# Half of the columns of the middle pass's row additions, moved from VectorE to GpSimd

## The reference, cut to what matters

```
terms = [x, L @ x]
for _ in range(2, 4):
    terms.append(2.0 * (L @ terms[-1]) - terms[-2])
out = einsum('kni,kio->no', stack(terms), weight)
```

```
deg = maximum(adj.sum(axis=1, keepdims=True), 1e-08)
```

## Time and profile before

| | us |
|---|---|
| median of 3 runs | 1737.84 |
| profiled execution | 1742.45 |
| its span, first to last instruction | 1740.6 |
| TensorE busy | 1542.5 (89%) |
| VectorE busy | 1250.4 (72%) |
| ScalarE busy | 947.7 (54%) |
| GpSimd busy | 297.3 (17%) |

### The profile page before, as it was taken

How to read it: one execution, slowest core, us unless ns; L and a number is a source line. 1 busy time by engine, 2 the same in 40 slices (tenths; PEclk the granted TensorE clock), 3 DMA queues, 4 the chain that set the end, 5 groups by cost and what they waited for, 6 DMA issues and landing times.

```text
span 1740.6 us, 21314 instructions
## 1 busy us (share of the span) xinstructions
PE 1542.5 (89%) x8169; PEld 653.1 (38%) x8214; DVE 1250.4 (72%) x1609; ACT 947.7 (54%) x920; POOL 297.3 (17%) x150
## 2 busy tenths in 40 slices
PE   6999989999999699999999997788788888888880
PEld 1433333333333344444444444233333333333330
DVE  4677699986888656747749654456567888888877
ACT  1233477753344433324343344656567999999964
POOL 1000000000000000000000002675224444444430
PEclk9999999999999799999999998999678999999995
DMA  9999599938999335333334302346124444544410
GB/s 349 412 413 413 213 357 381 392 130 316 413 413 381 115 146 193 147 146 146 145 135 156 145 1 73 121 133 218 37 97 133 148 155 136 186 163 158 136 46 24
DMA packets 118109, 348.99 MB, mean 201 GB/s; under 512 B 6324, under 2 KB 31224, under 8 KB 117752
## 3 DMA queue, kind: packets, MB, share of 16 engines
q1 hardware_dynamic: 106784, 329.27, 50.9%
q10 hardware_dynamic: 11224, 18.36, 2.8%
HBM read 329.78 MB, written 17.83 MB: 200 GB/s over the span
## 4 chain that ended last, share of the span: by engine, by line
PE 52%; issue 18%; DVE 13%; POOL 13%; ACT 2%; DMA 2%; SPq 0%; POOLq 0%; DVEq 0%; ACTq 0%
PE ps L741 13%; PE ps L863 13%; POOL ring L635 11%; PE ps L869 9%; DVE work L1611 4%; PE ps L674 3%; DVE work L1648 3%; PE ps L673 3%; PE ps L892 2%; POOL work L615 2%; PE ps L808 2%; DMA ring<-in_adjT 2%; PE ps L705 1%; PE ps L898 1%; DVE work L1624 1%
## 5 line engine op out<-in xcount | busy, mean ns | idle before, releaser
L615 POOL TENSOR_SCALAR work<-work 128x1024 int16<-128x1024 uint8 x32 | 97.0, 3041 | 1106.2 <-DMA work<-codes 1044.5
L863 PE MATMUL ps<-ring,X 128*64 128x512 f32 x512 | 264.0, 597 | 13.3 <-DVE ring L1867 13.3
L1134 ACT ACTIVATE work<-ps,code_bias 128x1024 uint8<-128x1024 f32 x128 | 135.8, 1111 | 247.7 <-PE ps L674 239.2
L864 PE MATMUL ps<-work,X 128*64 128x512 f32 x512 | 264.0, 597 | 0.0
L1255 ACT ACTIVATE work<-ring 128x2048 f32<-128x2048 f32 x64 | 122.2, 1911 | 222.0 <-PE ps L871 201.1
L635 POOL TENSOR_TENSOR ring<-ring,work 128x1024 f32<-128x1024 f32 x80 | 189.8, 2372 | 280.8 <-DVE work L2092 280.6
L871 PE MATMUL ps<-work 128*64 128x512 bf16 x768 | 208.2, 380 | 0.0
L869 PE MATMUL ps<-work 128*64 128x512 bf16 x768 | 208.2, 380 | 0.0
L958 PE MATMUL ps<-work 96*128 96x512 f32 x320 | 169.5, 655 | 0.0
L741 PE MATMUL ps<-ring,work 128*64 128x512 f32 x704 | 161.7, 601 | 0.0
L1864 DVE TENSOR_SCALAR work<-ring 128x2048 bf16<-128x2048 f32 x64 | 78.5, 1226 | 106.0 <-PE ps L871 105.8
(11 more groups left out here) (316 smaller groups left out, 2766.0 us busy)
## 6 DMA issues: line engine op xcount, KB each, us to landing
ring<-in_adjT SPq DMA_DIRECT2D x90, 2048.0 KB, 10.6
work<-in_adjT SPq DMA_DIRECT2D x26, 2048.0 KB, 12.0
ring<-in_adjT SPq DMA_DIRECT2D x48, 1024.0 KB, 7.7
codes<-work ACTq DMA_DIRECT2D x64, 256.0 KB, 6.1
work<-codes SPq DMA_DIRECT2D x32, 512.0 KB, 3.6
ring<-in_adjT SPq DMA_DIRECT2D x32, 512.0 KB, 3.6
X<-in_x ACTq DMA_DIRECT2D x1, 1024.0 KB, 6.9
work<-in_xT SPq DMA_DIRECT2D x2, 512.0 KB, 22.6
```

The source lines that it names most:

```text
L615: nc.gpsimd.tensor_scalar(decay[i % 2][:, 3, :].rearrange("p (h c) -> p h c", h=2), code_in[:, i % RING, :, 3, :], 128.0, None, ALU.mult). ...
L863: nc.tensor.matmul(ps[0:F, h, :], rows, ring[:, r, k, cols], start=start, stop=stop)
L864: nc.tensor.matmul(ps[F:P, h, :], rows, negs[:, pair, i, cols], start=start, stop=stop)
L1134: nc.scalar.activation(codes[:, u, k:k + 2, :].rearrange("p k c -> p (k c)"), ps[:, bank:bank + 2, :].rearrange("p k c -> p (k c)"), ACT.Relu,
```

## The change

In the middle pass VectorE adds columns 0 to 511 of each block and GpSimd columns 512 to 1023 (`ADD_COLS = HALF`), each to its own columns of the sums. GpSimd's additions stand in its program behind the constants. Each waits for its tile and for its own addition before; the first of all also waits for VectorE's 32 additions of the first pass. SP waits for GpSimd's additions too before it loads into a slot, and VectorE's first addition of the third pass waits for all 64. The semaphores of the square roots of the first two layers are merged into one.

```diff
@@ SP, wait_for_last_use
                 if t >= SLOTS:
                     sp.wait_ge(tile_signed, min(t + 1 - SLOTS, SLOTS))
+                    sp.wait_ge(pool_added, 2 * min(t + 1 - SLOTS, SLOTS))
@@ GpSimd, behind the constants
+            for a in tiles:
+                if a.p != 1:
+                    continue
+                waits_for_tile(pool, a)
+                if a.t == SLOTS:
+                    pool.wait_ge(row_added, SLOTS)
+                for i, k in enumerate(a.rows):
+                    if a.t > SLOTS or i:
+                        pool.wait_ge(pool_added, 2 * (a.t - SLOTS) + i)
+                    sums = row_sum[:, a.q, ADD_COLS:QC]
+                    nc.gpsimd.tensor_tensor(sums, sums, a.room[:, k, ADD_COLS:QC], ALU.add).then_inc(pool_added, 1)
@@ VectorE, add_rows
-                edges = a.room[:, k, :]
+                cols = slice(0, ADD_COLS if a.p == 1 else QC)
+                sums, edges = row_sum[:, a.q, cols], a.room[:, k, cols]
                 if rows_added[0]:
                     dve.wait_ge(row_added, rows_added[0])
+                if a.t == 2 * SLOTS:
+                    dve.wait_ge(pool_added, 2 * SLOTS)
                 if a.p == 0 and a.s == 0:
-                    ins = V.tensor_copy(row_sum[:, a.q, :], edges)
+                    ins = V.tensor_copy(sums, edges)
                 else:
-                    ins = V.tensor_tensor(row_sum[:, a.q, :], row_sum[:, a.q, :], edges, ALU.add)
+                    ins = V.tensor_tensor(sums, sums, edges, ALU.add)
@@ the roots of layers 0 and 1
-            nc.scalar.activation(stats[:, 4, :], stats[:, 3, :], ACT.Sqrt).then_inc(root0_made, 1)
+            nc.scalar.activation(stats[:, 4, :], stats[:, 3, :], ACT.Sqrt).then_inc(roots_taken, 1)
...
-                dve.wait_ge(root0_made, 1)
+                dve.wait_ge(roots_taken, 1)
...
-                nc.scalar.activation(stats[:, 4, blocks], stats[:, 3, blocks], ACT.Sqrt).then_inc(root1_made, 1)
+                nc.scalar.activation(stats[:, 4, blocks], stats[:, 3, blocks], ACT.Sqrt).then_inc(roots_taken, 1)
...
-                dve.wait_ge(root1_made, n + 1)
+                dve.wait_ge(roots_taken, n + 2)
```

More of the change, by code:

```diff
@@ L319, in adjacency_stack @@
         norm0_steps = sem("norm0_steps")
-        root0_made = sem("root0_made")
+        roots_taken = sem("roots_taken")
+        pool_added = sem("pool_added")
         normed = [sem(f"normed{l}") for l in range(3)]
@@ L350, in adjacency_stack @@
         var_made = [None] + [sem(f"var_made{l}") for l in (1, 2)]
-        root1_made = sem("root1_made")
         root2_made = sem("root2_made")
@@ L415, in adjacency_stack @@
         N_PUTS = 20
+        ADD_COLS = HALF
         GATE_STEPS = 25
```

## The result

The changed kernel takes 1760.16 us (median of 4 runs, 1757.65 to 1762.65) against 1738.38 for the kernel before: a ratio of 1.0129, 95% interval 1.0105 to 1.0154. It is slower by 22 us, where 23.5 were forecast (1761 us). The profiled run has a span of 1757.7 us; the trace of before has 1740.6.

The account below looks back on a forecast made before the run. VectorE was taken to bound the first layer's middle pass. 135.8 + 67.2 - 8 gave 195.0, plus 1.2 made 196.2 us against 172.7; the 23.5 us growth on the 1737.84 median gave 1761 us, range 1739 to 1783.

Parts of the forecast that it names:

- What bounds the pass: First layer's middle pass: VectorE bounds at 4.93 us per tile, TensorE just under at 4.56; the pass lasts 172.7 us.
- rival A: Middle pass: the engines don't hinder each other, TensorE bounds, pass 165 us, time 1730 us; chance 0.14.
- What is removed: VectorE's 64 middle-pass additions shrink from 1024 to 512 columns, saving 34.5 us and leaving 135.8 us.
- What is added: GpSimd does 64 additions of 128x512 in the middle pass, 1.24 us each, harmless by itself.
- What they share: Middle pass: a GpSimd addition excludes VectorE's two-input operations, and expectedly its mask, for nearly its whole length.
- The sum: Middle pass on VectorE: 64 holds of 1.05 us push in 67.2, 8 falls into waits, giving 195.0 us.
- The end of the pass: TensorE waits for every tile and ends 1.2 us after VectorE, making the middle pass 196.2 us.
- rival C: Middle pass: the whole GpSimd instruction excludes VectorE, nothing recovered, 43.7 us more, time 1782 us; chance 0.10.
- Edits at nothing: The new waits of loads, VectorE's third pass and GpSimd, and the merged square-root semaphore, add nothing further.
- Signs: Middle pass: VectorE additions above 0.69 us or masks above 2.29, GpSimd above 1.24, mask starts 5.6 to 5.9 apart.
- B: Middle pass: only reading is exclusive, 0.88 us per GpSimd addition, 4.6 to 12.6 us more, 1742 to 1750; chance 0.18.

Follow-up runs that it names:

- experiments 2: Changed kernel with GpSimd's 64 additions on a buffer nothing else uses then, half the columns missing from the row sums: 1755.49 us, ratio 1.0123.
- experiment 6: Changed kernel with each GpSimd addition replaced by a one-input doubling of the same 512 tile columns into an unused buffer: 1731.95 us, ratio 0.9961.
- experiment 5: Changed kernel with each GpSimd addition replaced by a memset of 1024 columns of an unused buffer: 1727.72 us, ratio 0.9954.
- experiment 4: Kernel before, without GpSimd: VectorE adds block 1 half in the first pass, half in the third, not in the middle: 1728.61 us, ratio 0.9954.

## Why the prediction was right, step by step

*What bounds the pass.* Right. Without GpSimd the pass fell to 164.0 us, where rival A had 165 from TensorE's rows, and the time to 1729.55 (A: 1730). That also prices what the split was worth had the engines been independent.

*What is removed.* 64 x (1.222 - 0.688) = 34.2 us; the prediction had 34.5.

*What is added.* GpSimd's addition alone takes 1.262 us (1.24 by halving L635, which is a multiplication of that form and not the addition that the prediction calls it).

*What they share.* Right in kind. The two rows that carried it, VectorE's L1522 held to the end of an L635 and the tiny L1763 held at the start of an L615, stand for what experiments 2, 5 and 6 show for these operations: reading is exclusive between GpSimd and VectorE's two-input operations, and VectorE's mask is excluded by writing too. The stretched L615 was no exception to be explained away: one input of 1024 held VectorE for 0.88 us, one of 512 in experiment 6 for 0.41 (median of those held). The rule of the Trainium skill (SBUF — State Buffer, "Who interferes with whom") agrees on which operations exclude each other, the write-only memset beside VectorE's additions among them; that the exclusion lasts for the whole instruction agrees nearly with GpSimd's additions (a hold of 1.06 us of 1.26), and not with its one-input operation (0.41 of 1.49).

*The sum.* The hold of 1.05 us was right: 1.06 where it shows. (Its working has a slip: by the row's own numbers L1522 got in at 1285.32 + 0.12 = 1285.44, 0.13 us before L635's end and not 0.08, which makes the hold 1.01 and the 67.2 us 64.6.) The net was 67.2 - 8 = 59.2 us pushed into VectorE; the stretching measured is 50.6. The mis-sized term is the part that falls where VectorE doesn't need the port: I took 8 us, half of what I had counted as possible, and it was 64 x 1.06 - 50.6 = 17 us. Six of GpSimd's 64 additions ran before VectorE's first mask of the pass. VectorE was occupied from 210.71 to 399.69, 189.0 us, where I had 195.0; of these, 3.0 it waited for TensorE's counts (L710), which I had not.

*The end of the pass.* Wrong, and by luck it made good most of that error. I had TensorE end 1.2 us after VectorE, since it would wait for every tile. But GpSimd, which runs ahead of VectorE, was through 18 us before the end; from 362 us TensorE was the chain, slowed at the turn before, and the next pass began 5.5 us after VectorE's last addition. 189.0 + 5.5 = 194.5, against 195.0 + 1.2 = 196.2. The sum had nothing for TensorE's clock, which stood under rival C alone; the fall to 0.50 lengthened TensorE's chain by 4.9 us just where it was the last. An estimate from that: at the full clock the pass would have been some 190 us and the change 17 us slower, not 22. No run tests it. So the mechanism was right, and that the number came within 2 us of the growth is partly luck.

*Edits at nothing.* Right as far as the runs show: experiment 5 keeps every new wait, with 64 instructions on GpSimd, and its pass is as short as without GpSimd (164.7 and 164.0 us).

*Signs.* L1628 and L621 far above 0.69 and 1.24, DMA share 0.74 (0.72 foreseen), TensorE waiting for VectorE before its counts, all other stages as before. L1665 starts 5.9 us apart on many plain tiles (5.6 to 5.9 foreseen), but from 3.9 to 8.05 over all of them.

*Rivals B and C.* B, reading alone and at L615's rate, gave 1742 to 1750; the time lies 10 us above it, though its idea of reading as the shared thing is what experiments 5 and 6 bear out. It was the rate that failed: 1024 reads held VectorE for 1.06 us in an addition of two inputs, where L615 had 0.88. The argument against B, that L1522 was kept out longer than 1.76 us, was of the same kind: 2048 reads at 1.06 for 1024 are 2.1 us. C's 79.4 us nowhere came about at 512 columns.

## What to carry to other kernels

Before work goes from VectorE to an idle GpSimd, look in the trace for a VectorE operation with two inputs in SBUF, or an f32 to bf16 mask like this one, that lies beside a GpSimd instruction, and compare it with its own median: two such rows carried this forecast. Where both engines read SBUF in two-input f32 additions, their times nearly add up (a hold of 1.06 us for a GpSimd addition of 1.26), and in this pass, which VectorE bounds, GpSimd's share cost VectorE more than it saved at each of the three splits tried. Look instead for a stage in which another engine bounds: the same 64 half-block additions were free in the passes that TensorE bounds, and that made the kernel 0.5% faster (experiment 4).

## What the runs showed of the hardware that I had not expected

- GpSimd's one-input f32 `tensor_scalar` of 512 columns takes at least 1.487 us, longer than its two-input addition of the same size (1.262), while it keeps a VectorE addition out for only 0.38 to 0.46 us, where it does so at all.
- A GpSimd memset (0.952 us for 1024 columns) doesn't touch VectorE's f32 additions (0.684 us beside it) but stretches the 128x4096 masks from 2.29 to 2.56 us on average (22 masks from the ring slots).
- Both engines wait: with 512 columns each, VectorE's additions averaged 1.31 us over the pass and GpSimd's 1.86, single ones of GpSimd up to 3.34.
- The hold comes in whole pieces: an addition of VectorE in the changed kernel took 0.69 us or at least 1.63, never a time between. The piece is 0.53, 1.06 and 1.61 us for 256, 512 and 768 columns of GpSimd's two-input addition.
